# Weight rounding on ScalarE, key norms summed in four column groups, and finer feed-forward waits in a four-part transformer kernel

## What is computed

```python
# 1 state-space block: u from the context, gate z from x
x1 = einsum(in_proj_w, ctx);  u = silu(conv4(x1) + conv_b)
dt_lo, B, C = split(einsum(x_proj_w, u));  delta = softplus(dt_proj_w @ dt_lo + dt_proj_b)
state = state * exp(delta * A) + (delta * u) * B;  y = state . C        # over 512 steps, 16 states
x = x + tanh(g) * ((y + D * u) * silu(layernorm(x)))
# 2 feed-forward with weights of three values and rows of 8 bits
gamma_w = clip(mean(|w|), 1e-5);  w_dq = clip(round(w / gamma_w), -1, 1) * gamma_w
gamma_x = clip(max|x| of the row, 1e-5);  x_dq = clip(round(x * 127 / gamma_x), -128, 127) * gamma_x / 127
x = x + tanh(g) * bit_linear(silu(bit_linear(h, gate)) * bit_linear(h, val), out)   # h = layernorm(x), 2048 wide
# 3 cross-attention, 16 heads of 128; keys and values from the context
q = rmsnorm(h @ Wq, gq);  k = rmsnorm(ctx @ Wk, gk);  x = x + tanh(g) * (softmax(q k^T / sqrt(128)) v @ Wo)
# 4 feed-forward with 4 experts, row n goes to expert n % 4
x = x + tanh(g) * ((silu(h @ gate) * (h @ up)) @ down)
```

## Time and profile before

| | us |
|---|---|
| median of 3 runs (2009.87 to 2034.65) | 2021.33 |
| profiled execution, its own time | 2014.32 |
| its span, first to last instruction | 2012.5 |
| PE busy | 1856.5 (92%) |
| DVE busy | 1386.6 (69%) |
| ACT busy | 936.6 (47%) |
| POOL busy | 616.6 (31%) |

### The profile page before, as it was taken

The page is one execution under the profiler, slowest core; times in us unless marked ns, Lnnn a source line. Parts: engine busy times, 40 slices in busy tenths (PEclk is TensorE's granted clock), DMA queues, the critical chain, the costliest instruction groups (busy, mean ns, idle before and its releaser), DMA issues.

```text
span 2012.5 us, 20103 instructions
## 1 busy us (share of the span) xinstructions
PE 1856.5 (92%) x6442; PEld 884.7 (44%) x6442; DVE 1386.6 (69%) x2076; ACT 936.6 (47%) x1848; POOL 616.6 (31%) x621
## 2 busy tenths in 40 slices
PE   7799998977998799999978999999998989999999
PEld 3355453433444234544433454444444434444543
DVE  4789876899996869988865999896764354431321
ACT  5856565544754355654624555654433333330100
POOL 1133321123644114454610335554312342320100
PEclk8789988988999889999988999999999999999999
DMA  6699952176775003887810257884101399874210
GB/s 236 210 265 284 275 181 101 53 202 154 195 194 140 12 22 94 206 207 186 205 56 18 58 152 180 243 199 117 43 21 59 112 277 272 254 208 183 94 52 32
DMA packets 159463, 304.40 MB, mean 151 GB/s; under 512 B 13944, under 2 KB 46968, under 8 KB 156416
## 3 DMA queue, kind: packets, MB, share of 16 engines
q1 hardware_dynamic: 140928, 236.01, 37.5%
q0 software_dynamic: 18432, 67.12, 17.2%
HBM read 177.64 MB, written 58.33 MB: 117 GB/s over the span
## 4 chain that ended last, share of the span: by engine, by line
PE 72%; DVE 11%; ACT 5%; issue 4%; DMA 4%; POOL 2%; SPq 1%; DVEq 0%; ACTq 0%; POOLq 0%
PE p L757 9%; PE p L710 8%; PE p L747 8%; PE p L727 8%; PE p L684 6%; PE p L794 6%; PE p L679 4%; PE p L600 4%; PE p L733 4%; PE p L691 3%; PE p L809 3%; PE p L645 2%; DMA s_U<-in_Wq 2%; PE p L581 1%; DVE s_U L1057 1%
## 5 line engine op out<-in xcount | busy, mean ns | idle before, releaser
L927 DVE TENSOR_TENSOR_SCAN s_M<-s_M 128x1024 f32<-128x1024 f32 x128 | 302.9, 2367 | 18.2 <-ACT s_M L1164 15.7
L1057 DVE CUSTOM_DVE_ANT_0 s_U<-p,s_U 128x512 f32<-128x512 f32 x256 | 187.3, 744 | 171.5 <-PE p L727 169.1
L727 PE MATMUL p<-s_U 128*128 128x512 f32 x512 | 269.3, 613 | 1.8 <-DMA s_U<-k_scratch 1.2
L710 PE MATMUL p<-s_U 128*128 128x512 f32 x512 | 254.7, 604 | 12.7 <-DMA s_U<-in_Wq 11.0
L1383 POOL DMA_DIRECT2D s_u<-s_M x128 | 113.5, 887 | 436.4 <-DVE s_M L932 395.7
L1427 POOL TENSOR_SCALAR s_U<-s_U 128x512 f32<-128x512 f32 x256 | 227.7, 913 | 5.9
L757 PE MATMUL p<-s_U 128*128 128x512 f32 x512 | 223.6, 592 | 0.0
L747 PE MATMUL p<-s_U 128*128 128x512 f32 x472 | 212.9, 594 | 2.4 <-DMA s_U<-p_scratch 1.6
L1294 ACT ACTIVATE s_U<-s_U 128x512 f32<-128x512 f32 x256 | 181.8, 719 | 57.4 <-DVE s_U L1061 57.4
L1299 ACT COPY s_U<-p 128x512 f32<-128x512 f32 x196 | 107.0, 591 | 173.8 <-PE p L733 170.3
L1164 ACT ACTIVATE s_M<-s_dl,s_small 128x511 f32<-128x511 f32 x256 | 170.3, 717 | 33.0 <-DVE s_M L927 32.8
(11 more groups left out here) (178 smaller groups left out, 2509.4 us busy)
## 6 DMA issues: line engine op xcount, KB each, us to landing
s_u<-s_M POOLq DMA_DIRECT2D x128, 512.0 KB, 7.3
s_bc<-bc_scratch SPq DMA_DIRECT2D x128, 256.0 KB, 4.9
k_scratch<-s_U SPq DMA_DIRECT2D x16, 1024.0 KB, 7.4
v_scratch<-s_U SPq DMA_DIRECT2D x16, 1024.0 KB, 6.3
s_U<-in_Wq SPq DMA_DIRECT2D x64, 256.0 KB, 7.8
s_U<-k_scratch SPq DMA_DIRECT2D x64, 256.0 KB, 5.0
s_U<-in_Wo SPq DMA_DIRECT2D x64, 256.0 KB, 4.3
s_U<-rk_scratch SPq DMA_DIRECT2D x64, 256.0 KB, 5.2
```

Source lines behind the costliest of these rows:

```text
L710: ins = e.matmul(banks[bk][:], wqq[j % 2][:, k, :], axT[b % 2][:, k, :], start=(k == 0), stop=(k == 3))
L727: e.matmul(banks[bk][:], qT[j % 3][:, k * 128:(k + 1) * 128], kT[j % 2], start=True, stop=True).then_inc(S["a_s"], 1)
L927: e.tensor_tensor_scan(w, dA[i % 2], w, 0.0, ALU.mult, ALU.add).then_inc(S["m_s"], 1)
L1057: e.tensor_tensor_reduce(out=Pm[j % 2][:, k, :], in0=banks[ABANK[kind, j, k]][:], in1=rkb[j % 2], scale=rq[:, k:k + 1], scalar=-3.0e38, op ...
```

## The change

- Weights: a new step `rnd` on ACT scales a piece and adds the rounding constant in one pass, DVE clips it in one pass (`clip`) instead of two, `put` on ACT is as before. `thr` is a step of its own. The planner's costs follow, the first loads get longer ones.
- Key norms: `n` is 4 matmuls of 512 columns, each with a stationary of 32 columns of ones, so that head h fills partitions 32h to 32h+31 of a bank, instead of 16 matmuls of one column. ACT copies the whole bank to SBUF (`nv`), four DMAs spread one row per head over 32 partitions of `krs` (`r`), POOL takes the power later (`pw`), and one DMA stores it (`st`). This is done for each of the 16 groups. The PE transpose, its copy and the 16 stores of 8 KB go.
- Feed-forward: the row maximum is taken piece by piece after each `m` (512 wide) and joined in `l` 0; the last cast of `l` 0 is cut in two halves that are signalled one by one; the first four transposes of `e` no longer wait for the small casts of the bias rows, only the fifth does. The planner's costs for `m` and `l` 0 change.
- Scores wait for the square of the queries instead of their copy; it is issued just behind.

```diff
-    QUANT += [("abs", w, c) for c in range(4)] + [("put", w, c) for c in range(4)]
+    QUANT += [("abs", w, c) for c in range(4)] + [("thr", w, 0)]
+    for c in range(5):
+        QUANT += [("rnd", w, c)] if c < 4 else []
+        QUANT += [("put", w, c - 1)] if c else []
+        QUANT += [("clip", w, c)] if c < 4 else []
...
-        KV += [(b, q, "k", i) for i in range(4)] + [(b, q, "v", 0)] + ([(NB - 1, q - 1, "r", 0)] if q and b == 0 else [])
-        KV += [(b, q, "v", 1), (b, q, "n", 0), (b, q, "v", 2), (b, q, "nv", 0), (b, q, "v", 3)]
-KV += [(NB - 1, 3, "r", 0)]
+        last = ((b - 1) % NB, q - (b == 0))
+        KV += [(b, q, "k", i) for i in range(4)] + [(b, q, "v", 0), (b, q, "v", 1), (b, q, "n", 0), (b, q, "v", 2), (b, q, "nv", 0)]
+        KV += [(*last, "pw", 0)] if q or b else []
+        KV += [(b, q, "v", 3), (b, q, "r", 0)] + ([(*last, "st", 0)] if q or b else [])
...
-                part(name, [("DVE", 1.6)], ("m", t, k - 1), free=pair)
+                part(name, [("DVE", 2.3)], ("m", t, k - 1), free=pair)
...
-            part(name, [("DVE", 5.4)], ("m", t, 7))
+            part(name, [("DVE", 3.6)], ("m", t, 7))
...
-            out.append(("Q", [("DMA", 5.0), ("ACT", 2.0)], [(0, "put", w - 1, c)] if w else [], (0, kind, w, c), [], []))
+            out.append(("Q", [("DMA", 5.0 if w else (17.0, 4.0, 9.0, 5.0)[c]), ("ACT", 2.0)], [(0, "put", w - 1, c)] if w else [], (0, kind, w, c), [], []))
+        elif kind == "thr":
+            out.append(("Q", [("DVE", 0.2), ("PE", 0.2), ("DVE", 1.0)], [(0, "abs", w, 3)], (0, kind, w, c), [], []))
+        elif kind == "rnd":
+            out.append(("Q", [("ACT", 2.0)], [(0, "thr", w, 0)], (0, kind, w, c), [], []))
+        elif kind == "clip":
+            out.append(("Q", [("DVE", 1.3)], [(0, "rnd", w, c)], (0, kind, w, c), [], []))
...
-        does = {"k": [("PE", 1.75), ("ACT", 1.2)], "v": [("PE", 1.75), ("ACT", 0.6)], "n": [("PE", 3.7)], "nv": [("ACT", 0.25), ("POOL", 3.0)],
-                "r": [("PE", 0.2), ("ACT", 0.3)] + ([("DMA", 8.0)] if q == 3 else [])}[kind]
-        needs = {"nv": [("K", at.get((b, q, "n", 0)))], "n": [("K", at.get((b, q, "k", 3)))], "r": [("K", at.get((b, q, "nv", 0)))]}.get(kind, [])
+        does = {"k": [("PE", 1.75), ("ACT", 1.2)], "v": [("PE", 1.75), ("ACT", 0.6)], "n": [("PE", 1.2)], "nv": [("ACT", 0.6)],
+                "r": [("DMA", 5.0)], "pw": [("POOL", 3.0)], "st": [("DMA", 8.0 if (b, q) == (NB - 1, 3) else 2.5)]}[kind]
...
+                            if i == 4:
+                                e.wait_ge(S["f_z"], 4 * b + t + 1)
...
-                        e.wait_ge(S["f_hq"], 4 * b + t + 1)
+                        e.wait_ge(S["f_hq"], 2 * (4 * b + t) + k)
...
-                            for t in range(4):
-                                ins = e.matmul(banks[bk][:, 4 * h + t:4 * h + t + 1], ksq[h][:, t * 128:(t + 1) * 128], ones[:, 0:1], start=True, stop=True)
+                            ins = e.matmul(banks[bk][32 * h:32 * h + 32, :], ones[:], ksq[h], start=True, stop=True)
...
-                            e.wait_ge(S["a_qc"], j + 1)
+                            e.wait_ge(S["a_qs"], j + 1)
...
-                        src = stg[c]
-                        e.tensor_scalar(src, src, thr[:, w:w + 1], 1.0, ALU.mult, ALU.min).then_inc(*v.up())
...
-                        e.tensor_scalar(src, src, -1.0, MAGIC, ALU.max, ALU.add).then_inc(S["q_rnd"], 1)
...
+                    elif kind == "clip":
+                        e.wait_ge(S["q_rnd"], 4 * w + c + 1)
+                        e.tensor_scalar(stg[c], stg[c], MAGIC - 1.0, MAGIC + 1.0, ALU.max, ALU.min).then_inc(S["q_cut"], 1)
...
+                n = src.shape[1] // len(done)
+                for i, up in enumerate(done):
+                    e.tensor_scalar(dst[:, n * i:n * i + n], src[:, n * i:n * i + n], MAGIC, 127.0, ALU.subtract, ALU.min).then_inc(*up)
...
+                        e.wait_ge(S["f_h"], i + 1)
+                        e.tensor_reduce(qt[:, 24 + ch:25 + ch], h[:, ch * 512:(ch + 1) * 512], AXX, ALU.max, apply_absolute_value=True).then_inc(*v.up())
...
-                        e.tensor_reduce(qt[:, 16:17], h, AXX, ALU.max, apply_absolute_value=True).then_inc(*v.up())
+                        e.wait_ge(*v.now())
+                        e.tensor_reduce(qt[:, 16:17], qt[:, 24:28], AXX, ALU.max).then_inc(*v.up())
...
+                    elif kind == "rnd":
+                        e.activation(stg[c], stg[c], ACT.Copy, bias=MAGIC, scale=thr[:, w:w + 1]).then_inc(S["q_rnd"], 1)
...
-                        e.activation(krs[:, 16 * b:16 * b + 16], banks[bk][:, 0:16], ACT.Copy, bias=EPS, scale=1.0 / HD).then_inc(S["k_nv"], 1)
-                    elif kind == "r":
-                        e.wait_ge(S["k_t"], q + 1)
-                        if q:
-                            e.wait_ge(S["d_rk"], 16 * NB * q)
-                        e.copy(rkt, banks[bk][0:64, 0:128]).then_inc(S["k_tc"], 1)
+                        if n:
+                            e.wait_ge(S["d_ksr"], 64 * n)
+                        e.activation(ksr, banks[bk][:], ACT.Copy, bias=EPS, scale=1.0 / HD).then_inc(S["k_nv"], 1)
...
+                        power(krs[:, 16 * n:16 * n + 16], (S["d_ksr"], 64 * (n + 1)), "k_p")
...
+                        e.wait_ge(S["k_nv"], n + 1)
+                        for h in range(4):
+                            e.dma_start(krs[32 * h:32 * h + 32, 16 * n:16 * n + 16],
+                                        ksr[32 * h:32 * h + 1, :].rearrange("o (p c) -> o p c", c=16)).then_inc(S["d_ksr"], 16)
+                    elif kind == "st":
+                        e.wait_ge(S["k_p"], n + 1)
+                        e.dma_start(rkd[j:j + 4].rearrange("h (p c) -> (h p) c", c=16), krs[:, 16 * n:16 * n + 16]).then_inc(S["d_rk"], 16)
...
```

More of the change, by code:

```diff
@@ L265, in weights @@
         if kind == "abs":
-            out.append(("Q", [("DMA", 5.0), ("ACT", 2.0)], [(0, "put", w - 1, c)] if w else [], (0, kind, w, c), [], []))
+            out.append(("Q", [("DMA", 5.0 if w else (17.0, 4.0, 9.0, 5.0)[c]), ("ACT", 2.0)], [(0, "put", w - 1, c)] if w else [], (0, kind, w, c), [], []))
[5 more added lines that the diff above has]
+            out.append(("Q", [("DVE", 1.3)], [(0, "rnd", w, c)], (0, kind, w, c), [], []))
         elif kind == "put":
-            out.append(("Q", ([] if c else [("DVE", 0.2), ("PE", 0.2)]) + [("DVE", 2.6 if c else 3.3), ("ACT", 2.0)], [(0, "abs", w, 3)], (0, kind, w, c), [], []))
+            out.append(("Q", [("ACT", 2.0)], [(0, "clip", w, c)], (0, kind, w, c), [], []))
         else:
@@ L376, in plan @@
             done[name] = ended[s, i, k]
-        if k == max(n for n, (on, _) in enumerate(does) if on not in ("POOL", "DMA") or len(does) == 1):
+        if k == max((n for n, (on, _) in enumerate(does) if on not in ("POOL", "DMA")), default=0):
             for x in gives:
@@ L540, in pe_quant @@
                 for kind, w, c in QUANT:
-                    if kind == "put" and c == 0:
+                    if kind == "thr":
                         e.wait_ge(S["p_set"], 8)
@@ L663, in pe_keys @@
                 for b, q, kind, i in KV:
-                    if kind == "nv":
+                    if kind not in "kvn":
                         yield
@@ new lines, in dve_quant @@
+                    if kind == "thr":
+                        e.wait_ge(S["q_abs"], 4 * w + 4)
+                        e.tensor_reduce(wab[:, 12 + w:13 + w], wab[:, 4 * w:4 * w + 4], AXX, ALU.add).then_inc(S["q_sum"], 1)
+                        e.wait_ge(S["q_mm"], w + 1)
+                        e.tensor_scalar(gam[:, w:w + 1], banks[6][:, 0:1], 1.0 / (DX * HID), EPS, ALU.mult, ALU.max).then_inc(*v.up())
+                        e.wait_ge(*v.now())
+                        e.reciprocal(thr[:, w:w + 1], gam[:, w:w + 1]).then_inc(S["q_thr"], 1)
+                        e.wait_ge(S["q_thr"], w + 1)
+                        if w < 2:
+                            e.wait_ge(S["d_raw"], 128)
+                            r = raw[:, 512 * w:512 * w + 512]
+                            e.tensor_scalar(r, r, thr[:, w:w + 1], None, ALU.mult).then_inc(S["q_raw"], 1)
+                    elif kind == "clip":
+                        e.wait_ge(S["q_rnd"], 4 * w + c + 1)
+                        e.tensor_scalar(stg[c], stg[c], MAGIC - 1.0, MAGIC + 1.0, ALU.max, ALU.min).then_inc(S["q_cut"], 1)
@@ L951, in dve_mamba, with quant_row @@
                     yield
-            def quant_row(src, amax, dst, sc, mul, last):
+            def quant_row(src, amax, dst, sc, mul, done):
                 e.tensor_scalar(sc[:, 0:1], amax, mul, EPS, ALU.mult, ALU.max).then_inc(*v.up())
@@ L1239, in act_keys @@
                 for b, q, kind, i in KV:
-                    n, bk = NB * q + b, KBANK[b, q, "n" if kind == "nv" else kind, i]
+                    n, bk = NB * q + b, KBANK.get((b, q, "n" if kind == "nv" else kind, i))
                     s = 2 * n + (kind == "v")
```

(9 more changed lines are left out.)

66 lines of the change are left out of this document (22 added, 44 removed).

## The result

The changed kernel takes 2006.97 us (median of 13 runs, 2001.85 to 2008.68), the one before 2022.34 in runs beside it: a ratio of 0.9925, 95% interval 0.9902 to 0.9949, so 15 us faster. (One of the 13 executions before took 3177.05 us, which doesn't move the median.) The forecast was 1988 us. The profiled execution has a span of 2006.9 us (2012.5 before).

The account below looks back on a forecast made before the run. TensorE was taken to bound the kernel, with only shifts of the attention's start at 472.19 us counting: 2012.5 - 14 - 0 - 6 - 7 = 1985.5 us of span, 1987.3 with 1.8 around it, forecast 1988; range 1964 to 2012.

Parts of the forecast that it names:

- The scans: 0: M(0)'s first to last scan: shorter key sums' gain and added work cancel, pace stays 5.35 us; bounds -19 and +10.
- From the last scan to F(0): 6 us off: Closing stage after M(0)'s last scan: shorter key sum before `yt` and earlier third weight gain 6 us; bounds -10 and +1.
- The start, -14: Before the first scan: reordered ScalarE passes bring it earlier, counted as 14 us off; bounds -18 and -8.
- F(0)'s first piece, -2: F(0)'s first piece on TensorE: 2 us earlier, as three key and value tiles and M(1)'s projections move.
- F(0), the rest of -7: From F(0)'s first piece to the attention's start: the remainder of F(0)'s 7 us gain, from key sums, projections and tail.
- Behind 472, 0: From the attention's start at 472 us to the end: no change; bounds -6 and +7.
- (b): M(0)'s scans: DMA load, ScalarE passes and clips lengthen the pace to 5.7 us, closing stage gains nothing; 2005 us; chance 0.13.
- (e): SP's queue in M(0): added issues delay loads of B and C, making the kernel slower; 2029 us; chance 0.07.
- (a): M(0)'s scans: DVE alone sets the pace, worth -19 us; 1969 us; chance 0.20.
- (c): Key sums on TensorE: column groups with 512 columns don't overlap, sum stays at 3.67 us; 1999 us; chance 0.03.
- (d): TensorE's clock: gaps in M(0) make it run cold before `yt` and in F(0), some 12 us; 2000 us; chance 0.09.
- The rule on small transfers: Key sums' DMAs: by the page, 80 small ones for 16 are the wrong trade, moving the sum towards its upper bound.

Follow-up runs that it names:

- quant_alone: Kernel before with only the weights' part of the change (rounding on ScalarE, one clip, new step order), planned anew; ratio 1.0072 to the kernel before.
- no_keys: Changed kernel with the key sums made as before, planned anew; weights and feed-forward as changed; ratio 1.0058 to the kernel before.
- ffn_alone: Kernel before with only the feed-forward's part of the change (split waits, reductions per piece, planner's costs); ratio 0.9983 to the kernel before.
- light_quant: Changed kernel with second and third weights cast in one pass, without rounding and clip (left out of the result); ratio 0.9915 to the kernel before.
- no_second: Changed kernel without the loads of the second weight (4 MB less, weight left out of the result), every engine step kept; ratio 0.9857 to the kernel before.
- half_v: Changed kernel storing only two of four heads' values per group (half the values left out of the result); ratio 0.9855 to the kernel before.
- keys_alone: Kernel before with only the key sums' part of the change, planned anew; ratio 1.0059 to the kernel before.
- one_spread: Changed kernel with a group's four spread DMAs made one, same packets and bytes; ratio 0.9886 to the kernel before.
- lean: Changed kernel with one spread DMA per group and one store per four groups, 20 issues in place of 80; ratio 0.9904 to the kernel before.
- two_buffers: Changed kernel with two buffers for the key sums in turn instead of one; ratio 0.9907 to the kernel before.
- old_sums: Changed kernel with its own plan kept, but key sums made as before by sixteen one-column matmuls; ratio 1.0118 to the kernel before.

## Why the prediction was wrong

It failed at **The scans: 0** and at **From the last scan to F(0): 6 us off**; that the kernel gets faster, and by less than 2%, held. By the profiles the terms missed by +0.5, +9.7, +10.0, -4.0 and +5.3 us, which is the 21.4 us between the span forecast, 1985.5, and 2006.9.

- **The start, -14:** -13.5 (71.31). Right, and by the reason given: quant_alone and no_keys start at 71.7.
- **The scans, 0:** +9.7. (Measured from ffn_alone, whose scans are those of before, it is +7.7.) The step let a gain from short sums cancel a cost of ScalarE's passes, clips and DMA load. ScalarE's passes and the clips cost nothing that could be measured (light_quant), and DVE's waits for ScalarE's decays did shrink, from 12.8 to 6.4 us (75 to 236 us). The step wrote that DMA work up to the last scan "is the same in less time, and it is at 99% already" and gave that no price of its own. Taken as the bound, it says that a start 13.5 us earlier can't bring the last scan much forward while the bytes before it stay: 63.6 MB were moved up to the last scan before, 62.5 after. The reordering that won the start also moved the second weight's loads from 45 to 64 us, where the engines had room, to among the scans. No run keeps the change and puts these loads back, so their share of the 9.7 us is argued (no_second) and not shown. What the runs show in place of the 0: waits for the loads of B and C, 14.1 us where it was 0.5, which go with the bytes (half_v).
- **The last scan to F(0), -6, with F(0)'s first piece, -2:** +2.0 together. The gain written for the key sum before `yt` came: from first to last `yt` it was 10.9 us and is 3.8; with the first `yt` 1.8 us later behind the gate that leaves 5.3 where the step took 4. The mean's wait went from 4.48 us to 0.49, but 2.5 us of waiting for the last magnitude sum came ahead of it. Missed was the single buffer of the sums: the new form makes ScalarE wait for a DMA, behind which stand evictions, a `put` and the silu. The prediction looked for what is queued behind SP's issues, not behind ScalarE's wait. The gate waits 9.9 us for it where it waited 0.4; two remedies bring that to 1.1 and 1.6.
- **F(0), the rest of -7:** from first piece to first queries 148.8 us became 139.8, -9.0 where -5 was written. The feed-forward's own edits don't account for it: in ffn_alone the stretch is 148.9 us, though TensorE's last wait for a cast fell from 11.0 to 8.3, and the ratio is 0.9983 with an interval that holds 1. In keys_alone and no_keys it is 134.8 and 129.3 under other plans. What did shrink is TensorE's work on the stretch's three key sums, from 12.1 to 3.2 us, and ffn_alone still has the 12.1. That the gain is theirs is likely, not shown.
- **Behind 472, 0:** +5.3 in the profile of after; but kernels with the same plan have 1541.9 (one_spread), 1543.5 (lean), 1549.3 (two_buffers) from first queries to end, before has 1540.3. All are above before's, by 1.6 to 9.0 us, and one profile of before is too little to tell that from 0.
- **Rivals.** (b), which had a chance of 0.13, is what happened: the pace it named, 5.7 us (5.66), a closing stage that gains nothing, and the time, 2005. Of its three causes DMA load is the one that the runs bear out. (e) set its own test, loads of B and C late by over 10 us in total: they were (14.1), but not through SP's issues, since 12.7 stay without the spread. (a) falls, DVE still waits among the scans. (c) falls by the 1.07 us, and of (d) only the attention's first eight matmuls were seen: 6.14 us at 461.34 where they took 3.67 before, 2.5 us, at a granted clock of 0.60 in place of 1.00. Between 254 and 472 us the clock is what it was (0.84 and 0.87; 0.83 and 0.86 before).
- **The rule on small transfers.** The Trainium skill, page "DMA: Bandwidth & Descriptors", section "Measured (HBM→SBUF, 128 partitions, SWDGE, issued from GpSimd)", has it that overhead dominates transfers under 64 KB. The 64 spreads cost 10 us (0.9925 against 0.9876 without them), and most came back with the same bytes in 16 DMAs (0.9886). As far as that goes the runs agree with the page, but the cost was far less than the sums won. It lies in how late the spreads land, by the gate's wait (9.91 and 1.62 us), not in SP's time.

no_keys' loss is not its plan's: the same sums in the changed kernel's plan (old_sums) are slower still. Not settled is what of keys_alone's loss is the plan and what the work, since no run made that kernel with another plan.

## What to carry to other kernels

When one resource is at 100% up to a point, count the work that must pass through it by then; an earlier start gains nothing for transfers that it only moves from before it to behind it. For a step that a change puts on an engine with a wait for a buffer, list what stands behind it on that engine, and give it a second buffer or a shorter way if something urgent does. And a part of a planned kernel that is tried alone also tries another plan: keep the plan fixed to learn what the work costs.

## What was not expected of the hardware

A DMA with source partitions 0, 32, 64 and 96 in one access works. For a group it holds SP 1.1 us in the mean of eight among the scans (9.0 in total in one_spread, up to 1.6 each, though 3.83 in one at 238.61), where four DMAs held it 5.2 (41.4 in total in after, up to 6.0). The four 2 KB DMAs issued from 240.34 to 245.73 had landed only at 259.55, 13.8 us later, with 1 MB loads queued around them. Between 265 and 286 GB/s came out of the DMA engines among the scans in every kernel but old_sums, whatever the issues.
